# Decoder layer, recurrence stage: the group's first product is added to the rows before the statistics of the rows two groups on

## The reference

```
x = x + recurrence(layernorm(x))             # this case
x = x + cross_attention(layernorm(x), ctx)   # 16 heads
x = x + butterfly_ffn(layernorm(x))          # 512 -> 2048 -> 512
```

```
step(z, u_t):  y = A * z + u_t ;  z_new = V y     # output 2 * real(z_new)
```

## Time and profile before

| | |
|---|---|
| median of 3 runs | 2285.23 us |
| lowest and highest run | 2284.19 and 2288.47 us |
| profiled execution, first to last instruction | 2285.0 us |
| TensorE busy in it | 2217.8 us (97%) |
| VectorE busy | 1696.3 us (74%) |
| ScalarE busy | 1227.2 us (54%) |
| GpSimd busy | 467.4 us (20%) |

### The profile page before, as it was taken

One profiled execution on the slowest core, in us unless ns is written; L12 is line 12 of the kernel. 1 busy time (PEld: TensorE's weight loads), 2 busy tenths in 40 slices (PEclk: granted clock), 3 DMA queues, 4 the chain that ended last, 5 costly groups with the idle time before them and its releaser, 6 DMA issues.

```text
span 2285.0 us, 41150 instructions
## 1 busy us (share of the span) xinstructions
PE 2217.8 (97%) x15910; PEld 1933.0 (85%) x15910; DVE 1696.3 (74%) x2854; ACT 1227.2 (54%) x2735; POOL 467.4 (20%) x578
## 2 busy tenths in 40 slices
PE   6998889999999999999999999999999999999999
PEld 4887677778878877778988989989989989889899
DVE  5666588888888888866857947858758669579567
ACT  2655566666676666554635535536446346355343
POOL 3531132222232222300030020200300300300203
PEclk8999999999999999999999999999999999999999
DMA  9888733332342332357676686785786676776765
GB/s 316 295 310 317 228 98 102 105 121 79 121 127 80 106 114 85 130 190 227 210 240 212 212 264 180 218 266 174 223 267 204 200 260 208 231 221 212 227 188 193
DMA packets 202090, 443.34 MB, mean 194 GB/s; under 512 B 32442, under 2 KB 70586, under 8 KB 200362
## 3 DMA queue, kind: packets, MB, share of 16 engines
q1 hardware_dynamic: 201898, 440.72, 60.0%
HBM read 341.66 MB, written 99.01 MB: 193 GB/s over the span
## 4 chain that ended last, share of the span: by engine, by line
PE 81%; ACT 8%; DMA 5%; DVE 4%; issue 1%; SPq 1%; POOL 0%; DVEq 0%; ACTq 0%; POOLq 0%
PE ps L441 69%; PE ps L1938 4%; DMA x_scratch<-xa 3%; PE ps L1906 2%; ACT es L1060 2%; ACT xn L906 2%; PE ps L1917 2%; PE ps L1869 1%; ACT wc_h L1016 1%; ACT pth L1034 1%; PE ps L1835 1%; DVE st L1256 1%; DMA wd_scratch<-stage 1%; DVE ptl L1293 1%; PE ps L1795 1%
## 5 line engine op out<-in xcount | busy, mean ns | idle before, releaser
L441 PE MATMUL ps<-ring,gh 128*128 128x256 f32 x3584 | 652.8, 284 | 0.1
L441 PEld LDWEIGHTS ps<-ring,gh 128*128 128x128 f32 x3584 | 558.3, 192 | 2.1 <-DVE gl L1293 1.5
L441 PE MATMUL ps<-xth,ring 128*128 128x512 f32 x1792 | 553.0, 389 | 0.0
L441 PE MATMUL ps<-ring,gl 128*128 128x256 f32 x1792 | 506.8, 283 | 0.0
L441 PEld LDWEIGHTS ps<-xth,ring 128*128 128x128 f32 x1792 | 336.4, 188 | 69.6
L1161 ACT ACTIVATE gh<-G 128x512 fp32r<-128x512 f32 x384 | 239.2, 629 | 218.7 <-PE ps L441 218.2
L441 PE MATMUL ps<-xtl,ring 128*128 128x512 f32 x896 | 348.6, 389 | 0.0
L441 PEld LDWEIGHTS ps<-ring,gl 128*128 128x128 f32 x1792 | 343.5, 192 | 0.0
L1293 DVE TENSOR_TENSOR gl<-G,gh 128x512 fp32r<-128x512 f32 x384 | 276.9, 733 | 50.5 <-ACT gh L1161 49.5
L849 POOL TENSOR_TENSOR es<-es,rinv 128x308 f32<-128x308 f32 x256 | 180.5, 736 | 422.0 <-DVE rinv L1467 422.0
L1144 ACT ACTIVATE G<-G,up_b 128x512 f32<-128x512 f32 x192 | 139.0, 724 | 221.9 <-DVE G L1579 221.9
(11 more groups left out here) (232 smaller groups left out, 4405.5 us busy)
## 6 DMA issues: line engine op xcount, KB each, us to landing
ring<-wup_scratch SPq DMA_DIRECT2D x224, 512.0 KB, 3.8
ring<-wdn_scratch SPq DMA_DIRECT2D x224, 512.0 KB, 3.6
X<-x_scratch SPq DMA_DIRECT2D x32, 1024.0 KB, 8.8
xa<-in_x SPq DMA_DIRECT2D x16, 1024.0 KB, 6.3
x_scratch<-xa SPq DMA_DIRECT2D x16, 1024.0 KB, 8.8
x<-x_scratch SPq DMA_DIRECT2D x16, 1024.0 KB, 5.5
x_scratch<-x SPq DMA_DIRECT2D x16, 1024.0 KB, 4.3
out_x<-X SPq DMA_DIRECT2D x15, 1024.0 KB, 7.8
```

Of the source, the lines that this page charges most:

```text
L441: mm = pe.matmul(bank, a, b, start=first and i == 0, stop=last and i == n - 1, skip_group_check=go_on)
```

## The change

In VectorE's turn g the first two subtractions of group g+1 and the add of product 0 now come first, and then the statistics of group g+2, with the other two subtractions as callbacks of `moments`. The adds of products 1 to 3 follow as before. In the last two turns the order stays what it was. No instruction is added or removed.

```diff
             for g in range(NG):
                 lows = [lambda c=c: lo1_piece(g + 1, c) for c in range(KC)] if g + 1 < NG else []
-                if g + 2 < NG:
-                    stats1(g + 2, [lows[0], lows[1], None, None])
-                    lows = lows[2:]
-                elif g == NG - 2:
-                    lows[0]()
-                    lows[1]()
-                    lows = lows[2:]
+                for low in lows[0:2]:
+                    low()
+                lows = lows[2:]
                 for c in range(KC):
                     n = KC * g + c
...
                     V.tensor_tensor(xs, xs, ps[:, 4 + n % 2, :].rearrange("p (b t n) -> p b t n", b=2, t=T), ALU.add).then_inc(x1_ready, 1)
                     if c == 0:
-                        for low in lows:
-                            low()
+                        if g + 2 < NG:
+                            stats1(g + 2, [lows[0], lows[1], None, None])
+                        else:
+                            for low in lows:
+                                low()
```

## The result

The changed kernel takes 2308.35 us (median of 4 runs, 2305.34 to 2311.25), the kernel before 2286.85 us (4 runs on the same chip, 2284.19 to 2290.66). The ratio is 1.0086, with a 95% interval of 1.0069 to 1.0102: slower by 0.9%, where 2308 us and 1.0% were forecast. The profiled executions span 2309.4 and 2285.0 us, 24.4 us apart, against 21.5 us between the medians: the one of the changed kernel is the slowest of its four, 2311.25 us. (A run's time is some 1.9 us more than the span of its trace.)

What follows compares the result with a forecast made beforehand. TensorE, busy 97% of 2285.0 us, was taken as the bound. Terms 13.7 + 3.3 + 3.3 - 3.4 + 3.4 + 3.4 - 1 = 22.7 us gave 2308 us, 1.0% slower, range 2293 to 2329.

Steps and rivals of the forecast that it cites:

- turns 0 and 1, clock included: Recurrence turns with 6 pieces: +3.3 us each from later statistics and tiles, and +3.4 us for the clock in both.
- turns 2 to 12, clock included: Eleven recurrence turns of 13.3 us, 146.3 against 132.63: +13.7 us; clock +3.4 us, 1.7 in two of twelve turns.
- turn 13: Recurrence turn with 5 pieces: 14.1 us against 17.5, as the regrouped weights would come in time: -3.4 us.
- Part (a): VectorE: the two subtractions ahead of the statistics cost nothing, covered by the 2.2 us of piece and product.
- Part (b): VectorE: add of product 0 no longer stands behind a late load; gain at most 7.8 us, in 4 places.
- Part (c): Statistics start 3.99 us later, in a closed chain from transposes through add and tiles to next transposes: turn 2.5 us longer.
- the room: Turn 6: tiles reach TensorE with 0.65 us to spare for the first transpose, about 1.5 for the last eight.
- The late loads: Longer turns let row loads land in time; turn 5's load, for which VectorE waits 5.75 us, fits by 0.8 us.
- The clock: TensorE waits lower its clock: +3.4 us for turns 0 and 1, +3.4 us for the other 12 turns (range 0 to 20).
- The rival with the clock down in most turns: Clock falls in ten or more turns at 1.7 us each: 39.7 us slower, 2325 us; chance 0.18.
- The end: Last two turns: some of ScalarE's 1.58 us wait for stores of copies may go; -1 us taken.
- the bound of -1.6 us: Last two turns: larger bound on the gain from ScalarE's store waits ahead of the last piece; the other bound is 0.

Runs made afterwards that it cites:

- store moved: Changed kernel with SyncE issuing the store of group 2 ahead of the 4 MB of regrouped weights instead of behind them: 2307.09 us, ratio 1.008.

## Why the prediction was right

The sign, the size and the mechanism came as forecast. By its terms, measured from end of transposes to end of transposes in the profiled executions. The last column is the changed kernel with the store moved, whose turns are otherwise the same:

| part | forecast | changed kernel | store moved |
|---|---|---|---|
| turns 0 and 1, clock included | +3.3 +3.3 +3.4 | +5.2 and +6.4 | +11.1 in both |
| turns 2 to 12, clock included | +13.7 +3.4 | +19.2 | +17.7 |
| turn 13 | -3.4 | -3.4 | -3.4 |
| from turn 14 to the first attention matmul | -1 | -2.9 | -2.9 |
| the start | 0 | +0.4 | -1.4 |
| sum | 22.7 | 24.9 (24.4 at the end of the span) | 21.1 |

The transposes of turns 0, 1, 2, 13 and 14 end at 56.0, 74.6, 93.4, 245.2 and 259.4 us, before at 55.6, 69.0, 81.4, 214.0 and 231.5; the first attention matmul starts at 298.5 us, before at 273.5. With the store moved, those of turns 0, 2, 13 and 14 end at 54.3, 91.1, 241.4 and 255.5 us, and attention starts at 294.6. The turns' lengths are the differences. Between the medians the change costs 21.5 us.

**Part (a), the early subtractions:** right for this change, where the statistics stand behind the add anyway and VectorE waits 0.96 us between the subtractions and the add. Alone, ahead of the statistics, they do lengthen a turn, from 10.79 to 11.92 us.

**Part (b), the early add:** right that at most 7.8 us were there; the run with the change's order in turns 5 and 8 to 10 only adds that this order gets none of it on balance.

**Part (c), the closed chain:** this was the decision, and it held to 0.1 us in the turn, and again with 1.2 us (half of the statistics) taken out of it. The reading that gave it was to ask of the moved work not whether its engine has time (VectorE was busy for 8.02 of 10.79 us) but when its last consumer needs it: the move was 3.99 us and the room less. Of the two values given for the room, only the 1.5 us ahead of the last eight transposes is one. The 0.65 is measured to the wrong consumer: the first eight need only tiles 0 and 1, which are ready at 137.16 + 1.52 = 138.68 us, 2.5 us ahead of them. The sum went by the last eight, so nothing hung on it, and 3.99 less the turn's 2.55 gives 1.44 us of room.

**The late loads:** right that a longer turn lets them land, worked out with 0.8 us to spare in turn 5. The changed kernel has no wait for a load, and moving the store changed nothing in it.

**Turn 13:** -3.4 us on both sides; the run with the subtractions alone shows -3.9 there.

**The clock** is the term that was mis-sized. I took 1.7 us for each of turns 0 and 1, and two drops in the others. Turn 0 did lose that, 0.19 of 9 us, but turn 1 twice as much, 0.31 of 11:

```profile
64.00:73.00 9.00, 5.71 (x29) 4.30 (x29) 2.61 (x12) 4.49 (x7) 6.87 (x11) 0.81 0.78 244
82.00:93.00 11.00, 7.72 (x38) 6.54 (x37) 2.64 (x8) 4.55 (x8) 8.72 (x23) 0.69 0.48 174
```

With the store moved it is the other way round, 0.38 of 9 us in turn 0 and 0.28 of 6 in turn 1:

```profile
64.00:73.00 9.00, 6.25 (x25) 5.22 (x26) 1.08 (x2) 4.49 (x7) 8.18 (x14) 0.62 0.90 275
...
85.00:91.00 6.00, 5.56 (x30) 5.02 (x31) 0.69 (x1) 3.13 (x6) 5.14 (x17) 0.72 0.38 145
```

So waits of the same length, 3.3 us, cost 1.7 us or 3.4, and together 5.1 in both traces where 3.4 stood; about 0.5 us of these 5.1 in the changed kernel falls into the waits themselves and lengthens nothing. Of the eleven turns 2 to 12 three had a drop in the changed kernel's trace and two in the other, at 1.6 us each: 4.9 or 3.2 us where 3.4 stood. That is 10 us in all in the changed kernel's trace where 6.8 stood, 8.3 in the other. Without their drops turns 2 to 12 are 14.3 us longer than before, not 13.7; turns 3 and 12 take 13.6 us. The rival with the clock down in most turns fell: eight and nine of the eleven have none. The section of the Trainium skill beside it (TensorE: Matmul & The Clock Gate, "A second HAM failure mode: psum-queue depth-cycling") describes a clock that goes down and up again with the iterations. With TensorE idle for 13.34 - 11.47 = 1.9 us of a turn in three pieces, these traces show it in three and two turns of eleven.

**The end** was mis-sized the other way. ScalarE waits for no stored copy of a piece there any more, and TensorE's waits between turn 14 and attention, 1.09, 1.03, 0.21 and 2.25 us before, are a single one of 2.23; the bound of -1.6 us counted the last piece alone.

In the changed kernel's trace turns 0 to 12 are 3.7 us over their terms and the end 1.9 us under its own. These errors went against each other, so the sum is nearer to the result than its terms are to theirs, and that much of the agreement is luck. So is the base: the forecast added 22.7 us to a span, 2285.0 us, and took it for a time, which is some 1.9 us more. By differences the forecast is 22.7 us, and 21.5 us were measured.

## What to carry to other kernels

When a step is put behind another on the same engine, follow its result to the last consumer and back to the step that it is now put behind: if that closes a ring, each turn takes at least the ring's length, and idle engines don't help. The room before the change is the shortest distance between a result and its own consumer, read in a turn that waits for nothing. An engine's wait behind a late load is no gain waiting to be had if the load paces the turn anyway; then the order of the transfers is where the time may be, and a transfer that is moved later still needs its time to land before its first use. A turn of the expected length proves no chain: look at who released whom.

## What the runs showed of the hardware that was not expected

TensorE's clock can go down though no wait ahead of it is as long as 1 us. Ahead of the drop at 174 us in the changed kernel the product waited 0.22 us, the first eight transposes 0.84 and the last eight 0.80:

```profile
169.96 0.39 PE L441 MATMUL ps<-rh,xt1h 128*128 128x256 f32 x1 [0.22 <-DVE xa L1353]
172.38 1.09 PE L1766 MATMUL ps<-ident,xn 128*128 128x128 f32 x8 [0.84 <-ACT xn L918]
```

The same three waits stand in the turns before and after with no drop. Among turns 2 to 12 three had one in this trace, two in the one with the store moved, one in the one with turns 0 and 1 undone. With a doubled piece in each turn, which takes the first wait away and cuts the second to 0.4 to 0.6 us in most turns, none had one; that is one execution, and with one drop in another that had all the waits it is a hint and no proof.
